# A three-layer interaction tower in fp32: which tiles are split into rounded parts, on which engine, and in which order

## The reference

```python
x0 = xk = inputs                              # (1024, 39, 16)
for idx, (W, b) in enumerate(params):         # three layers, 128 outputs each
    z = jnp.einsum('bhd,bkd,hks->bsd', x0, xk, W) + b[None, :, None]
    z = jax.nn.relu(z)
    if idx != n_layers - 1:
        half = z.shape[1] // 2
        xk = z[:, :half, :]                   # 64 go on
        direct.append(z[:, half:, :])         # 64 are outputs
    else:
        direct.append(z)
logit = jnp.sum(jnp.concatenate(direct, axis=1), axis=-1)
...
h = jnp.maximum(h @ W_top1 + b_top1, 0.0)
h = jnp.maximum(h @ W_top2 + b_top2, 0.0)
y = h @ W_top3
```

## Time and profile before

| | |
|---|---|
| median of 3 runs | 1279.92 us (1279.79 to 1281.16) |
| profiled execution | 1279.59 us, span 1277.7 us |
| granted TensorE clock, mean | 0.996 |
| busy: TensorE | 1197.3 us, 94% |
| VectorE | 1074.4 us, 84% |
| GpSimd | 1015.7 us, 79% |
| ScalarE | 586.4 us, 46% |

### The profile page before, as it was taken

The page is one execution under the profiler, slowest core; times in us unless marked ns, Lnnn a source line. Parts: engine busy times, 40 slices in busy tenths (PEclk is TensorE's granted clock), DMA queues, the critical chain, the costliest instruction groups (busy, mean ns, idle before and its releaser), DMA issues.

```text
span 1277.7 us, 15242 instructions
## 1 busy us (share of the span) xinstructions
PE 1197.3 (94%) x3912; PEld 730.6 (57%) x3912; DVE 1074.4 (84%) x915; ACT 586.4 (46%) x592; POOL 1015.7 (79%) x639
## 2 busy tenths in 40 slices
PE   0378999999999999999999999999999999999899
PEld 0145665656565665656566665656566565656555
DVE  2268998989899898989999898989989898999762
ACT  1144444454544445444544445454444445454443
POOL 6788888888888898888888888888888885656571
PEclk9989999999999999999999999999999999999999
DMA  5681826436190825528191734619082643734000
GB/s 121 224 276 45 295 70 232 142 124 249 44 328 7 281 90 185 189 77 296 25 323 28 244 129 140 234 48 325 7 297 72 210 163 90 279 104 147 0 1 1
DMA packets 81243, 196.26 MB, mean 154 GB/s; under 512 B 23983, under 2 KB 35342, under 8 KB 81193
## 3 DMA queue, kind: packets, MB, share of 16 engines
q1 hardware_dynamic: 70953, 193.14, 43.7%
q0 software_dynamic: 10240, 2.64, 2.5%
HBM read 193.17 MB, written 12.78 MB: 161 GB/s over the span
## 4 chain that ended last, share of the span: by engine, by line
PE 39%; POOL 38%; issue 18%; DVE 3%; ACT 1%; POOLq 0%; DVEq 0%
PE acc L867 36%; POOL lo L465 23%; POOL emb L455 14%; DVE prod L746 2%; ACT hi L605 1%; DVE hi L756 0%; DVE lo L759 0%; POOL pairs_r L485 0%; PE xk L918 0%; PE acc L918 0%; PE acc L945 0%; DVE wlo L735 0%; PE acc L921 0%; PE xk L921 0%; PE xk L934 0%
## 5 line engine op out<-in xcount | busy, mean ns | idle before, releaser
L746 DVE TENSOR_TENSOR prod<-x_tiles,xk 128x1024 f32<-128x1024 f32 (+2 forms) x643 | 756.5, 1215 | 139.0 <-PE acc L867 77.9
L465 POOL TENSOR_TENSOR lo<-prod,hi 128x1024 fp32r<-128x1024 f32 (+1 forms) x288 | 688.1, 2392 | 164.6 <-ACT hi L605 159.7
L867 PE MATMUL acc<-prod,wfull 128*128 128x512 f32 (+2 forms) x1408 | 662.3, 595 | 0.0
L605 ACT ACTIVATE hi<-prod 128x1024 fp32r<-128x1024 f32 (+1 forms) x291 | 308.2, 1060 | 379.2 <-DVE prod L746 296.0
L867 PEld LDWEIGHTS acc<-prod,wfull 128*128 128x128 f32 (+2 forms) x1408 | 265.9, 190 | 205.7 <-issue 175.0
L867 PE MATMUL acc<-hi,whi 128*128 128x512 f32 (+1 forms) x800 | 352.9, 441 | 25.3 <-ACT hi L605 25.3
L455 POOL DMA_INDIRECT emb<-table,block_idx x320 | 309.6, 968 | 66.5 <-issue 54.8
L867 PE MATMUL acc<-lo,whi 128*128 128x512 f32 (+1 forms) x736 | 312.6, 513 | 15.5 <-POOL lo L465 15.4
L867 PE MATMUL acc<-hi,wlo 128*128 128x512 f32 (+1 forms) x800 | 315.9, 395 | 0.0
L867 PEld LDWEIGHTS acc<-lo,whi 128*128 128x128 f32 (+1 forms) x736 | 137.6, 189 | 149.1 <-issue 92.3
L867 PEld LDWEIGHTS acc<-hi,whi 128*128 128x128 f32 (+1 forms) x800 | 150.8, 188 | 80.3 <-issue 43.9
(11 more groups left out here) (76 smaller groups left out, 210.9 us busy)
## 6 DMA issues: line engine op xcount, KB each, us to landing
x_tiles<-x_rows SPq DMA_DIRECT2D x304, 512.0 KB
x_rows<-x_rows SPq DMA_DIRECT2D x16, 624.0 KB
x_tiles<-x_rows SPq DMA_DIRECT2D x32, 256.0 KB
x_stack<-x_rows SPq DMA_DIRECT2D x48, 156.0 KB
emb<-table,block_idx POOLq DMA_INDIRECT x320
x_rows<-x0T SPq DMA_DIRECT2D x64, 32.0 KB
x_tiles<-w SPq DMA_DIRECT2D x1, 768.0 KB
x_tiles<-w SPq DMA_DIRECT2D x1, 704.0 KB
```

The lines of the kernel that those rows point to most:

```text
L465: nc.gpsimd.tensor_tensor(lo[0:r, product_slot(j), :], prod[0:r, product_slot(j), :], hi[0:r, part_slot(j), :].bitcast(f32), ALU.subtract) ...
L605: nc.scalar.activation(hi[0:r, part_slot(j), :], held(n, parity, j)[0:r, :], ACT.Copy).then_inc(hi_ready, 1)
L746: nc.vector.tensor_tensor(held(n, parity, j)[0:r, :], in0, in1, ALU.mult).then_inc(product_ready, 1)
L867: mm = nc.tensor.matmul(z[:, c], w[0:r], part[0:r, c], start=first and i == 0, stop=last and i == len(weights) - 1)
```

## The change

The strings of kinds are replaced. Layer 0 has three G instead of two. Layer 1 has seven G instead of eight and five D instead of three. Layer 2 has eight G as before and three D instead of two. In all, eight D a block instead of five and 19 F instead of 22; G (18) and H (2) keep their number. Since the G of the last block stand at other tiles, the places at which GpSimd splits the top network's operands are named anew.

```diff
-KINDS = ["GFFGFFF", "GFDGF" * 2 + "GFHGF" + "GFDGF", "GFFGF" + "GFFGD" + "GFHGF" + "GFDGF"]
+KINDS = ["GFGFGFF", "GFDGFDGFDGFGHGFDGFDF", "GFGFGFGFGDGFHGFDGFDF"]
...
-                    after = {} if l == 1 else {3: split_top, 8: split_logits, 15: lambda: split_top1(0, 1),
-                                               18: lambda: split_top1(1, TILES1)}
+                    after = {} if l == 1 else {4: split_top, 8: split_logits, 13: lambda: split_top1(0, 1),
+                                               16: lambda: split_top1(1, TILES1)}
```

## The result

The changed kernel takes 1310.06 us (median of 4 runs, 1308.3 to 1311.91) against 1279.88 us before. The ratio is 1.023, with an interval of 1.022 to 1.025. The forecast was 1308.

A forecast was written before the change was run, and what follows sets the result against it. TensorE was taken to set the 72.8 us block, with VectorE having 1.4 us to spare in layer 1. The terms 21 + 1.2 - 0.6 + 0.8 + 3 + 3 = +28.4 on 1279.59 gave 1308.0 us, range 1284 to 1322.

The forecast's parts named there:

- (a): TensorE: three F a block become D, 1.0 us less a block, 70.8 us unstalled.
- (b): VectorE in layer 1: added subtracts make lo 18 late before F19, a stall of 2.2 us, 2.3 with the restart.
- rival 1: VectorE's wait for its own subtract costs nothing: block 73.6 us, time 1297 us; chance 0.14.
- the lead is cut at product 4: VectorE, layer 1: product 4 needs the slot of layer 2's last F, so starts 0.5 us after TensorE begins the layer.
- (c, d): GpSimd: layer 1 stall of 1.8 us inside (b)'s; layer 2's lo 8 late, 1.3 us with restart.
- Block: One block of three layers takes 74.4 us, 1.6 more than 72.8: +21 us over 13 gathering blocks.
- Start: First layer 1, bound by GpSimd with one more lo in the prologue: layer 0 begins later, +3 us.
- End: Top network: one more lo ahead of split_logits, +3 us; last layers before it +1.2, -0.6 and +0.8.
- a late lo costs its lateness and 0.1 us: Price of a TensorE wait for a late lo, read from the old stall at G15 of layer 1.
- rival 2: GpSimd keeps up in layer 2, only VectorE's stall stays: block 73.1 us, time 1291 us; chance 0.14.
- What the profile would show: Period near 74.4, VectorE without idle in layer 1, waits at named tiles, TensorE busy down 16 us, clock as before.
- The other side: VectorE's and GpSimd's leads both suffice, lo 18 in time: block 70.8 to 71.5 us, time 1261 us; chance 0.12.

The follow-up runs named there:

- the two kernels with all remedies: Changed kernel and kernel before, each with gathers dealt out anew, subtracts one tile behind their products, sum behind layer 0's products: 1255.05 and 1264.23 us.
- after_nogather: Changed kernel with only the rows of blocks 0 to 2 gathered and reused by later blocks: 1319.22 us, ratio 1.032.
- l02_alone: Kernel before with only the kinds of layers 0 and 2 changed, layer 1 keeping its three D: 1289.18 us, ratio 1.007.
- after_spread: Changed kernel with the same 20 gathers a block dealt out differently among the G, so that GpSimd is never late: 1314.43 us, ratio 1.027.
- l1_alone: Kernel before with only the kinds of layer 1 changed, layers 0 and 2 as before: 1296.42 us, ratio 1.014.
- after_all3: Changed kernel with gathers dealt out anew, subtracts one tile behind their products instead of two, sum behind layer 0's products: 1255.05 us, ratio 0.982.
- two together: Changed kernel with gathers dealt out anew and subtracts one tile behind their products, sum still ahead of layer 0's first product: 1273.64 us, ratio 0.995.
- after_sumlate_nogather: Changed kernel, only rows of blocks 0 to 2 gathered, sum over d moved behind layer 0's products: 1309.71 us, ratio 1.023.
- after_early18_nogather: Changed kernel, only rows of blocks 0 to 2 gathered, layer 1's subtract of D18 moved ahead of the sum: 1289.98 us, ratio 1.008.

## Why the prediction was right, point by point

- **TensorE's own work (a).** Right: 1.0 us a block and 70.8 us unstalled, shown by the two kernels with all remedies.
- **VectorE's chain in layer 1 (b).** Right in place and size, but one premise does not hold. In the changed kernel the waits of layer 1 are, from the rows: lo of G11 should start at 618.77 + 2.18 + 0.92 = 621.87 and starts 0.96 late, G13 0.66, D18 0.44, and 0.1 each for the restart, together 2.4 us; forecast 2.3. The wait of a product for the subtract in front of it is there again (606.01 to 607.35, 1.34 us), so rival 1, in which it costs nothing, does not hold. The premise is that the lead is cut at product 4, by its slot. Product 4 (second of the row 603.75) starts without waiting; VectorE has run without rest since 589.40 in layer 2, where it waited for the slot of the late G8. That product 4 starts 0.5 us behind TensorE, as forecast, is luck: in `after_nogather` it is 0.96 us (532.66 against 531.70), VectorE's last wait is at 511.33, and D18 is 2.58 us late instead of 2.2.
- **GpSimd in layers 1 and 2 (c, d).** Right in the changed kernel: lo of G8 of layer 2 was due 0.23 us after the last hi matmul (587.28), at 587.51, and starts 1.12 us late, 1.2 with the restart; forecast 1.3. `l02_alone` shows a case that the chain leaves out: it can begin at G0 of layer 0. In the changed kernel GpSimd does rest before G4 of layer 0, since the late D18 holds back its hi; it starts G4 5.4 us after TensorE starts the layer, forecast 5.5.
- **Block.** 74.42 us against 74.4, so +21.1 us over 13 blocks; forecast +21.
- **Start.** Layer 0 behind the first layer 1 begins at 115.03 against 112.20: +2.8, forecast +3.
- **End.** Under-sized. From the last transposes to the last layer 2 (which starts at 1234.90, before at 1206.89) it is 144.8 us against 140.0, +4.8, where I had +1.4 (1.2 - 0.6 + 0.8): there the stall of D18 is one gap again, 2.35 us at 1153.95, and the clock is 0.83 from 1150 to 1160 us. The last layer 1 waits 1.27 us, for GpSimd's lo (1217.85) and not for VectorE's. From the last layer 2's start to the end it is 75.2 against 70.8, +4.4 for +3. In all, the profiled execution (1311.91 us, the slowest of four) is 32.4 us longer in its span, for +28.4; the medians differ by 30.2.
- **The step that was wrong**: that a late lo costs its lateness and 0.1 us, whatever its size, so that GpSimd's stall in layer 1 "lies inside" VectorE's and the layer loses 2.3 us once. The price was read off stalls of 0.7 us. At 1.9 and 2.4 us in one piece a stall costs about 1.5 us more most times. In the changed kernel GpSimd's late lo cut the 2.4 us into three pieces, so the step cost nothing in 13 blocks, and that was luck; it shows only once, at the end. In `after_spread`, where GpSimd is in time in both layers, the same working gives the 73.1 us of rival 2 and some 1291 us, and it takes 1314. Rival 2 itself, with GpSimd in time in layer 2 alone, was not run; in `l1_alone` the waits of layer 1 are cut in three (0.66, 0.49 and 0.20 us), and it loses 2.2 us there (73.67 against 71.5 unstalled) with the clock at 1.00, where 2.3 were forecast.
- **What the profile would show.** The waits stand where they were forecast, and VectorE has no idle time in layer 1. TensorE's busy time is not down 16 us: it is 1200.7 us against 1197.3. The four groups that come late start 3.2 us late a block, of which the records show 2.5 as idle time; with 0.1 us each for the restart, 1.1 us of waiting a block count as busy, 14 us in 13 blocks. The granted clock is 0.990 on average, before 0.996; in the blocks it is 1.00.
- **A slip in the range.** The low end does not follow from its terms: 1291 less 2 for start and end and less 13 x 0.2 is 1286, not 1284. Nothing hangs on it.
- **The other side** (both leads suffice) had the right condition: with VectorE's and GpSimd's chains in time (`after_all3`) the block is 70.83 us, as that rival has it, and the time 1255 us; it had 1261.

What stays open: each remedy's worth in `after_all3` apart from the others, since they were not all run singly with gathers, and a part of what the end of the run loses (4.8 and 4.4 us).

## What to carry to other kernels

Before moving work to an engine, count its work in the stage where it has the least to spare, from the point at which its lead is bounded, and follow it to the instruction that another engine wants: a busy share over the whole run (84% here) did not show it. Stalls of several engines at one place hide each other. Removing one alone, with the gathers in, showed nothing or made it worse (1312 to 1317 us against 1310), two together gave 36 us, the three 55 us; so judge a remedy with the others in place. And an instruction that looks like a delay may be the cover of the next wait, as the sum was.

## What the runs showed of the hardware

The granted clock depends on how the waiting is cut. One gap of TensorE of 2.33 to 2.43 us a block was followed by matmuls at the lower level, 1.2 GHz, in 26 of 28 cases (`after_nogather` and `after_spread`; the mean of the window of 10 us is 0.83 where the slow stretch lies in one), about 1.5 us of loss each. Gaps of 1.89 to 1.92 us were in 10 of 13 cases; one of 1.82 us (1143.84 in `l1_alone`) and one of 1.73 us (1155.84 in `after_sumlate_nogather`) were not (1.00). Waits of 0.95, 0.79, 0.50 and 0.26 us in the same 75 us were not, nor were the 14 of 1.35 to 1.36 us in `after_early18_nogather`. The longer gap of 3.09 us in the first layer 1 of the changed kernel was followed by the low clock too:

```profile
100.97 1.22 PE L867 MATMUL acc<-lo,whi 128*128 128x512 f32 x2 [3.09 <-POOL lo L465]
101.99 0.63 PE L867 MATMUL acc<-hi,whi 128*128 128x512 f32 x1
...
104.45 0.40 PE L867 MATMUL acc<-hi,wlo 128*128 128x512 f32 x1
```

The matmuls take 0.63 us until 103.7 and 0.40 us after that. The Trainium skill (TensorE: Matmul & The Clock Gate, section "Part 1: The HAM clock gate (the "warmup" mystery)") says that a monitor of TensorE's activity sets the clock and that its phase is not tied to the kernel; the equal gaps of 1.9 us with different clocks behind them agree with that. The runs set no threshold: gaps of 1.9 and of 2.4 us come both with and without the low clock.
